# Attention and MX FFN on one core: probabilities transposed in two DMAs a head, query rows by 128 through DMA, FFN weights returned in twelve pieces

## What is computed

```python
x = x + _L0_xattn_ref(_layernorm(x), ctx_2048, Wq, Wk, Wv, Wo)     # 16 heads of 128
x = x + _L0_ffn_ref(_layernorm(x), w_gate, w_up, w_down)           # 512 -> 2048 -> 512

# attention
q = (inputs_q @ Wq).reshape(b, sq, H, HD) * (1.0 / np.sqrt(HD))
attn = jax.nn.softmax(jnp.einsum('bqhd,bkhd->bhqk', q, k), axis=-1)
ctx = jnp.einsum('bhqk,bkhd->bqhd', attn, v).reshape(b, sq, H * HD)
return ctx @ Wo

# FFN; both operands of each product are rounded in blocks of 32 with a shared power of two
gate = _mx_linear(x, w_gate)
up = _mx_linear(x, w_up)
return _mx_linear(jax.nn.silu(gate) * up, w_down)
```

## Time and profile before

| | |
|---|---|
| three runs | 2155.86 us median, 2154.7 to 2156.72 |
| the profiled execution | 2156.28 us, its span 2154.7 us |
| TensorE busy | 2069.8 us, 96% of the span |
| vector, scalar, POOL busy | 1538.8 us, 1024.8 us, 795.3 us |
| mean granted clock of TensorE | 0.991 |
| attention part, FFN part | about 1770 us, about 385 us |

### The profile page before, as it was taken

The page is one execution under the profiler, slowest core; times in us unless marked ns, Lnnn a source line. Parts: engine busy times, 40 slices in busy tenths (PEclk is TensorE's granted clock), DMA queues, the critical chain, the costliest instruction groups (busy, mean ns, idle before and its releaser), DMA issues. The chain is left out here.

```text
span 2154.7 us, 47837 instructions
## 1 busy us (share of the span) xinstructions
PE 2069.8 (96%) x15818; PEld 1530.8 (71%) x15818; DVE 1538.8 (71%) x3455; ACT 1024.8 (48%) x2760; POOL 795.3 (37%) x1093
## 2 busy tenths in 40 slices
PE   6899999999999999999999999999999978899996
PEld 5678788787878787878787878888788853344442
DVE  6777777777777777777777767776665547988884
ACT  7765555454555555545454545554444432222331
POOL 4323333333333333333333333331111005777774
PEclk9999999999999999999999999999999999999998
DMA  6743333333333333333333333332323253454554
GB/s 218 183 85 74 77 77 77 77 77 74 77 75 77 77 77 77 77 77 77 75 79 77 77 63 77 77 72 65 60 63 64 52 152 67 80 91 85 85 90 68
DMA packets 398590, 179.26 MB, mean 83 GB/s; under 512 B 361984, under 2 KB 374784, under 8 KB 398400
## 3 DMA queue, kind: packets, MB, share of 16 engines
q1 hardware_dynamic: 375616, 125.10, 29.2%
q0 software_dynamic: 16608, 45.36, 8.4%
q10 hardware_dynamic: 6176, 6.29, 1.0%
HBM read 61.08 MB, written 27.26 MB: 41 GB/s over the span
## 5 line engine op out<-in xcount | busy, mean ns | idle before, releaser
L562 ACT ACTIVATE qk<-b_qk 128x512 f16<-128x512 f32 x256 | 152.7, 596 | 607.9 <-PE b_s L1011 607.9
L860 DVE TENSOR_REDUCE nmax<-b_s 128x2 f32<-128x512 f32 x257 | 177.7, 691 | 334.7 <-PE b_s L1011 308.9
L1011 PE MATMUL b_v<-attn_weights,kvT 128*128 128x256 f16 x3072 | 377.2, 273 | 8.5 <-POOL attn_weights L392 8.5
L1011 PE MATMUL b_qk<-xT,attn_weights 128*128 128x256 f16 x3072 | 380.8, 274 | 1.8 <-DVE xT L708 1.7
L1011 PE MATMUL b_qk<-kvT,attn_weights 128*128 128x256 f16 x3072 | 378.3, 273 | 0.0
L884 DVE SCALAR_TENSOR_TENSOR psplit<-prob,rrec,psplit 128x256 f16<-128x256 f32 x514 | 287.2, 600 | 80.1 <-ACT psplit L603 80.1
L1011 PEld LDWEIGHTS b_v<-attn_weights,kvT 128*128 128x128 f16 x3072 | 300.3, 98 | 44.2 <-issue 9.5
L1011 PEld LDWEIGHTS b_qk<-xT,attn_weights 128*128 128x128 f16 x3072 | 302.2, 98 | 39.1 <-DVE xT L708 2.4
L1011 PEld LDWEIGHTS b_qk<-kvT,attn_weights 128*128 128x128 f16 x3072 | 301.3, 98 | 35.5
L603 ACT ACTIVATE psplit<-prob,rrec 128x256 f16<-128x256 f32 x514 | 233.0, 500 | 109.8 <-DVE rrec L877 109.3
L593 ACT ACTIVATE prob<-b_s,nmax 128x256 f32<-128x256 f32 x514 | 239.2, 470 | 56.1 <-DVE nmax L860 26.9
(11 more groups left out here) (124 smaller groups left out, 2747.3 us busy)
## 6 DMA issues: line engine op xcount, KB each, us to landing
ffn_w<-wffn SPq DMA_DIRECT2D x48, 256.0 KB, 3.1
acc<-xtok POOLq DMA_DIRECT2D x16, 512.0 KB, 4.2
out<-acc POOLq DMA_DIRECT2D x16, 512.0 KB, 3.8
out<-attn_weights POOLq DMA_DIRECT2D x32, 256.0 KB, 4.5
xrow<-xq POOLq DMA_DIRECT2D x61, 128.0 KB, 3.7
kvrow<-kvt POOLq DMA_DIRECT2D x61, 128.0 KB, 3.3
stage<-wattn SPq DMA_DIRECT2D x12, 512.0 KB, 4.0
ffn_scratch<-ffn_t SPq DMA_DIRECT2D x48, 128.0 KB, 1.8
```

The costliest lines, as they stand in the source:

```text
L562: eng.activation(dst, src, ACT.Copy, scale=scale).then_inc(sm[done], 1)
L860: eng.tensor_reduce(nmax[:, :], bS[:, :].rearrange("p (q f) -> p q f", q=2), AX_X, ALU.max, negate=True).then_inc(sm["max_done"], 1)
L1011: last = eng.matmul(out, l, r, start=(a == 0), stop=(a == len(pairs) - 1))
```

## The change

It does these things.

- **Probabilities**: `transpose_p` issues one DMA transpose for each query tile of 128 as soon as that tile's low half is written; the first of them also waits for the context product. The semaphore counts 32 a head.
- **Query rows**: loaded by 128 (from `xtok`; `xq` is gone), once in two quads. Statistics in the first head of an even quad, normalised in its fourth, high half by the scalar engine at that head's end, low half in the first head of the odd quad, both into `xsplit`; SP transposes `xsplit` into `xT` by one DMA in the second head of the odd quad. TensorE's transposes are gone, and it waits for `xT` once a batch.
- **POOL's prep**: an even quad computes the deviation and doesn't wait for the normalised rows; an odd one waits for them and loads the next.
- **FFN weights**: twelve transfers of four tiles (512 KB), two a head in quad 62 and one a head in quad 63, into chunk 1 and the first half of chunk 2; the FFN's buffers move to what is free in chunks 0 and 2.
- **First x tiles of the FFN**: both are issued in the last quad, behind its first and second head's transposes.
- **`x_clip`** of a batch's second tile comes two heads earlier.
- **Loops**: the first four quads are written out on the scalar and the vector engine; the scalar engine's and SP's loops run over two quads.

The core of the diff:

```diff
             def transpose_p(i, half_):
 
-                wait_apart(eng, "p_lo", i + 1)
-                wait_apart(eng, "c_done", i + 1)
-                eng.dma_start_transpose(probT[:, :].rearrange("p (j f) -> p j f", j=8),
-                                        half(psplit, half_, 1024)).then_inc(sm["pt_loaded"], 16)
+                for q in range(2):
+                    wait_apart(eng, "p_lo", 2 * i + q + 1)
+                    if q == 0:
+                        wait_apart(eng, "c_done", i + 1)
+                    eng.dma_start_transpose(half(probT, q).rearrange("p (j f) -> p j f", j=4),
+                                            half(psplit, 2 * half_ + q)).then_inc(sm["pt_loaded"], 16)
+
+            def transpose_x(m):
+
+                wait_apart(eng, "x_lo", m + 1)
+                eng.dma_start_transpose(xT[:, bass.ds(((m + 2) & 3) * 1024, 1024)].rearrange("p (j f) -> p j f", j=8),
+                                        xsplit[:, :]).then_inc(sm["xT_loaded"], 16)
...
                 for k in range(QUAD):
                     transpose_p(4 * n + k, k % 2)
+                    if m is not None and k == 1:
+                        transpose_x(m)
...
+            for k in range(QUAD):
+                transpose_p(4 * (NQ - 1) + k, k % 2)
+                if k < 2:
+                    load_x_tile(k, k)
+            transpose_p(4 * NQ, 0)
...
-            load_x_tile(0, 0)
-            transpose_p(4 * NQ, 0)
-            load_x_tile(1, 1)
...
-            def prep(r):
-                rstd(ROWS, 1, "aggr_done", "rstd_step", "rstd_done", r)
-                wait_apart(eng, "xn_ready", r + 1)
-                load_x(r + 1)
+            def prep(r, m, odd):
+                if odd:
+                    wait_apart(eng, "xn_ready", m + 1)
+                    load_x(m + 1)
+                else:
+                    rstd(P, 1, "aggr_done", "rstd_step", "rstd_done", m)
...
             def x_prep(m):
-                hi(prep_slot(xT, m + QPB, 0), bX[:, 0:KC * ROWS].rearrange("p (c f) -> p c f", c=KC), X_SCALE,
-                   "x_tr", m + 1, "x_hi")
+                if not isinstance(m, int) or m > 0:
+                    eng.wait_ge(sm["xT_loaded"], 16 * m)
+                hi(x_part(0), xnorm[:, :].rearrange("p (c f) -> p c f", c=KC), X_SCALE, "xn_ready", m + 1, "x_hi")
...
+                    if resident:
+                        w0, each, done = resident
+                        for a in range(each):
+                            load_resident(w0 + 4 * (each * k + a), n, done)
...
             eng.wait_ge(sm["ffn_stored"], 16 * FFN_TILES)
-            load_resident(0, 32, NQ - 1, "gate_up_resident")
-            quad(NQ - 1, prepare=False)
-            load_resident(32, FFN_TILES, NQ, "down_resident")
+            quad(NQ - 2, prepare=False, resident=(0, 2, "gate_up_resident"))
+            quad(NQ - 1, prepare=False, resident=(32, 1, "down_resident"))
...
-                if q == 4 and k == 3:
+                if q == 4 and k == 1:
                     x_clip(2 * b + 1)
...
-                    if prepare and k == 0:
-                        x_stats(n)
+                    if prepare and k == 0 and odd:
+                        x_lo(m)
+                    if prepare and k == 0 and not odd:
+                        x_stats(m)
...
-                    if prepare and k == 3:
-                        x_lo(n)
+                    if prepare and k == 3 and not odd:
+                        x_apply(m)
...
-                    if prepare and k == 1:
-                        x_apply(n)
...
-                    if prepare and k == 2:
-                        x_transpose(n)
```

More of the change, by code:

```diff
@@ L141, in build, with free_part @@
         first_kv_rows = first[:, 4 * D:4 * D + QPB * KC * ROWS]
[L143 to L159, removed]
+        def free_part(chunk, part, pc, pieces):
+            at = chunk * 2 * WCHUNK + part * WCHUNK + pc * PIECE
+            return wall[:, at:at + pieces * PIECE]
+        inter = free_part(2, 1, 0, 4).bitcast(F32)
+        iqT = free_part(2, 1, 4, 4).bitcast(BF16)
+        sil = free_part(0, 0, 0, 2).bitcast(F32)
+        iq = free_part(0, 0, 3, 2).bitcast(BF16)
+        i8 = free_part(0, 0, 5, 1).bitcast(FP8)
+        dsum = free_part(0, 1, 0, 2).bitcast(F32)
+        xqT = free_part(0, 1, 3, 1).bitcast(BF16)
         i_amax, i_pow, i_inv = [sb(f"inner_{a}", 32, F32)[:, :] for a in ("amax", "pow", "inv")]
         i_scale = sb("inner_scale", 32, BF16)[:, :]
-        FW = 2 * 2 * WCHUNK
+        FW = 2 * WCHUNK
         fw = wall[:, FW:FW + FFN_TILES * 512].bitcast(BF16)
@@ L207, in prep_slot, with x_part @@
             return v[:, bass.ds((m >> 1) & 3, 1), bass.ds(m & 1, 1), part, :, :].rearrange("p u z c f -> p (u z c) f")
+        def x_part(part):
+            return xsplit[:, :].rearrange("p (c h f) -> p h c f", c=KC, h=2)[:, part]
         def attn_w(n, part, off, size):
@@ L295, in ffn_quad, with odd @@
                         load_ffn(w + 1)
+            def odd(n):
+                return (n - 1) // 2 if n % 2 and n < NQ - 4 else None
             for n in range(QPB):
@@ L304, in _ @@
             ffn_quad(FFN_FROM, store=False)
[L305 to L313, removed]
+            ffn_quad(FFN_FROM + 1, m=odd(FFN_FROM + 1))
+            with eng.Fori(FFN_FROM // 2 + 1, FFN_TO // 2 - 1) as m:
+                ffn_quad(2 * m)
+                ffn_quad(2 * m + 1, m=m)
+            for n in range(FFN_TO - 2, FFN_TO + 2):
+                ffn_quad(n, store=(n <= FFN_TO), load=(n < FFN_TO - 1), m=odd(n))
+            with eng.Fori(FFN_TO // 2 + 1, NQ // 2 - 2) as m:
+                ffn_quad(2 * m, store=False, load=False)
+                ffn_quad(2 * m + 1, store=False, load=False, m=m)
             def load_x_tile(t, at):
@@ L322, in load_x_tile @@
                                         ).then_inc(sm[f"xqT_loaded{at}"], 16)
+            for n in range(NQ - 4, NQ - 1):
+                ffn_quad(n, store=False, load=False)
+            for k in range(QUAD):
[3 more added lines that the diff above has]
+            transpose_p(4 * NQ, 0)
             def transpose_inner(v, at):
@@ L854, in quad @@
                 w = n - FFN_FROM
+                m, odd = 2 * s + q // 2, q % 2
                 ends = q == QPB
@@ L937, in _ @@
                 split_piece(0, pc)
-            quad(0, split=QUAD)
-            with eng.Fori(1, QPB - 1) as n:
-                quad(n, split=QUAD)
-            quad(QPB - 1, split=QUAD // 2)
+            for n in range(QPB):
+                quad(n, split=QUAD // 2 if n == QPB - 1 else QUAD, s=0, q=n)
             quad(FFN_FROM, ffn=True, s=0, q=QPB)
@@ L1012, in product @@
                 return last
-            def x_transpose(m):
-                eng.wait_ge(sm["xn_ready"], m + 1)
-                wait_apart(eng, "x_lo", m)
-                for c in range(KC):
-                    last = eng.transpose(bX[:, c * ROWS:(c + 1) * ROWS], xnorm[:, c * P:(c + 1) * P],
-                                         ident[0:ROWS, 0:ROWS])
-                last.then_inc(sm["x_tr"], 1)
             def ffn_rhs(tile0, c):
```

111 lines of the change are left out of this document (57 added, 54 removed).

## The result

The changed kernel took 2105.62 us, median of 4 runs (2102.65 to 2108.13), beside 2155.28 for the kernel before (4 runs, 2154.55 to 2156.72): a ratio of 0.9768, interval 0.9751 to 0.9785, 50 us less. The forecast was 2102.5.

A forecast was written before the change was run, and what follows sets the result against it. TensorE was taken as the bound, busy 396.7 of 400 us in attention. Terms 29.4 + 10 + 13.3 + 1 = 53.7 us off 2156.3 gave 2102.6, stated as 2102.5; own range 2094 to 2113, widened to 2092 to 2125 for two rivals.

The forecast's parts named there:

- Query rows by 128: TensorE's query-row transposes go to DMA, so each of 60 quads' projections starts 0.49 us sooner: 29.4 us won.
- The first four quads: At the start, TensorE's waits for POOL and for the probabilities lose their cause: 10 us won, ends 4 and 14.
- The split: Probabilities in two transposes: second half lands 0.2 to 0.5 us later, inside the slack; middle heads taken as 1 us won.
- 1.5 us of slack is left: nothing in a normal head: In a normal head the later second half still lands 1.5 us before the context product needs it: no cost.
- the jump of the vector engine's loop: Late contexts once a batch in the middle: ends 12.4 us won or 6.5 lost, taken as 1 us won.
- The return of the weights: Last two attention quads: avoiding the 4 MB transfer's wait and half clock wins 7.3 us; the pieces lose 2.
- my end of 6: Upper bound for the returned weights' pieces: four heads of quad 62 each late by 1.5 us, 6 us lost.
- The turn to the FFN: From the last attention projection to the FFN's third product: 19.05 us becomes 11.1, 8.0 us won, ends 3 and 9.5.
- The x tile's place in the queue: The first FFN x tile, issued behind head 255's transpose, cost a 6.31 us wait; loading it earlier removes that.
- Only TensorE's part: Rival, 0.11: scalar engine's splitting and transposes under the pieces take over the start's and end's waits; 2125 us.
- A jump of the scalar engine's loop costs: Rival, 0.10: each of 24 jumps of its longer loop makes a head wait 0.82 us, 20 us lost; 2122 us.
- Halves in series: Rival, 0.07: second half's data waits for the first's landing, 0.7 us late in 256 heads, 180 us lost; 2283 us.

## Why the prediction was right, and where it was not

**Direction and size.** 2105.6 against 2102.5, within the forecast's own range. The bound was read rightly: what left TensorE left the span. That the sum came so near is in part luck: by the profiled execution the start, the split and the weights' return brought 5.6, 9.7 and 5.5 us less than forecast, and a relief at the vector engine's loop that I had put at 1 was 15 or more and paid for most of it.

**Query rows by 128 (29.4): right.** The transposes alone gave 28.8. What replaces them was not tried alone; with it and one transpose a head TensorE waits 0.4 us in the middle, so it costs nothing there that shows.

**The first four quads (10): the cause right, the price given back in part.** POOL's wait alone was worth 9.5 to head 16, as forecast. With the 2 us of the f32 transposes the stretch should have gained 12 and gained 6.4. SP still stands 19.1 us on POOL's pieces, and TensorE's 5.5 us of waits for the probabilities, which I had said lose their cause, became 7.6. One transpose a head gained 7.5 there, but the variants whose edits lie elsewhere spread from 6.4 to 7.8 too, so the split explains at most 1, and about 4 us stay open. The timeline has the contexts late here with the scalar engine splitting weights just before; I named it as what is late next, and no run isolates it.

**The split (nothing in a normal head, +1 with the loop's edge): wrong twice, the errors opposite.** The step that failed is "1.5 us of slack is left: nothing in a normal head". The 0.4 us was right, and so is the slack of the median head (1.45); but slack has to be held against the longest landings, not the median one. At the two places of a batch where POOL moves 512 KB, landings reach 4 to 6 us, and the later, second half meets it: the loss was 12 us. Between heads 16 and 240, where I had put 6.5 at most, it was 9.7 by the changed kernel's profiled execution and 7.4 to 9.4 by the four variants whose edits lie elsewhere. The page "DMA: Bandwidth & Descriptors" of the Trainium skill (rules for kernel authors) says to coalesce many small transfers into one large. By that rule the split only loses, and the runs agree, with 12 us; I was wrong to put the loss inside the slack.

The other error hid this one. For the jump of the vector engine's loop I took 1 us of relief out of 12.4. The changed kernel lost the whole stall but for one gap, and the same relief in the kernel before is worth 15. I had looked for the cure in the work behind the jump (a clip moved, a statistics pass less); the run with the loop shifted puts it, for the kernel before, in the place of the code; for the changed kernel the place and the shorter pass are not told apart. By the stretch of heads 16 to 240: the kernel with one transpose gained 43.4 there, 16.0 above the f32 transposes' 27.4, as the shifted loop had gained 16.2; the split took 9.7 of it (less in the four variants), and 6.3 were left where I had 1.

**The return of the weights (7.3 − 2): the gain right, the loss mis-sized.** The bulk transfer's 7.3 went, but the pieces cost 1.49 + 2.10 + 1.86 = 5.45 us of waits and, at the lower clock, about 0.5 + 1.2 more: 7.2 in all, above my end of 6. I had set a piece against the slack and left out that the issuing engine decides the order: two pieces ahead of two halves take from the halves' landing what the later start had left, and one of the waits brought the clock down with it, which is chance in part: with the vector engine's loop shifted the same head waited 2.08 us and the clock stayed up.

**The turn to the FFN (8.0): the sum right, its parts less so.** From the projection's end to the third product 5.6 us were gained, not 8.0: the last two projections ran at the lower clock, 2.74 and 2.77 us where 1.47 is normal, after waits of 2.15 and 0.94. The remaining 2.6 lie almost all behind it, in the FFN, were not forecast, and are hardly more than the spread of this stretch. The x tile's place in the queue, which I had made the reason, is worth 1.2 us there once the 2 MB transfer is gone, and the transfer 1.7 once the place is early; the other 2.7 of the 5.6 come with either.

**The rivals.** *Only TensorE's part* is out: POOL's wait alone gave 10. *A jump of the scalar engine's loop costs* is out: the loop is the same with one transpose a head, and between 160 and 1640 us TensorE waited 0.4 us. *Halves in series* is out for the changed kernel, and ran slower when made true; its 180 us were 121.5, as not every head reached that point.

## What to carry to other kernels

Hold a slack against the longest landing in the stretch, and look for the transfers of other queues that recur with it. Splitting a transfer whose issue costs the same in halves buys an earlier first half, which nobody waits for, and pays with a later second one, which somebody does. When an engine idles for "issue" where its loop jumps back, move the loop's place in the code before changing its work: it is a cheap experiment, and in the kernel before it was worth 0.7%. Transfers that fill a gap belong in the queue whose small, urgent transfer they must not overtake.

## What the hardware showed that I had not expected

- The place of a loop in one engine's code moved the whole kernel by 15 us (0.9926), and two gaps after a jump, 2.6 and 1.8 us, hurt where one of them didn't.
- A transpose of half the data was issued in the same time (1.2 us) and landed 0.6 us earlier (2.4 and 3.0), alone; beside a store of 512 KB it took 4.9 where the full one took 3.8.
- After TensorE's waits of 2.10 (the changed kernel) and 2.21 us (the kernel before) its next 4 us ran at the lower clock, which cost 1.7 us, and after 2.15 and 0.94 close together its next 5.5, which cost 2.8. After 1.49 and 1.86 it did not, nor after 2.08 (changed, vector loop shifted), 2.16 (one transpose a head), 2.19 (x tiles late), 2.23 (the kernel before) and 2.25, twice (POOL's pieces first). The length of the wait alone does not tell the two apart.
